# Mamba block with routed experts: expert rows scattered to a DRAM row of their own and summed at the end, in place of accumulating scatters

## The chip, the cores and the metric

The kernel runs on one core of a Trainium2 chip. The metric is the device time of one execution in microseconds (us); lower is better. All data are float32 unless a shape says otherwise.

## The reference, cut to what matters

4096 tokens (8 batches of 512) of width 128 pass a layer norm, and then two things that are added to the input: a bidirectional Mamba block, and a mixture of 16 experts of which each token takes 4.

```python
xn = _layernorm(x)
x = x + mamba(xn) + experts(xn)

def experts(x):
    logits = -sum((x - keys) ** 2) + x @ rw + rb
    topv, topi = top_k(logits, 4)
    w = softmax(topv)
    hidden = gelu(x @ w1[e] + b1[e])
    exp_out = hidden @ w2[e] + b2[e]
    return sum(w[k] * exp_out[topi[k]] for k in range(4))
```

Only the chosen experts are worked out. So each token has four expert rows of 128 numbers, made at four different places of the program, and their sum is one of the three addends of the output.

## The kernel before, in words

**Preparation (0 to about 243 us).** Tokens are normalised and routed. Each pair of token and choice gets a slot in a DRAM table `slots_d`, sorted by expert and padded to tiles of 256 rows (80 tiles). GpSimd copies the normalised rows there with 128 indirect DMAs (L817), in 16 groups; ahead of each group `tag` (L803 to L808) writes the gate weight beside the row. The row's other extra word is the token's number, written once by an iota for all tokens (L776). Unused slots carry numbers below `UNUSED`, so what they yield goes to rows that nobody reads. In the same stretch TensorE, ScalarE and VectorE prepare the Mamba inputs of all batches and SP stores them to DRAM.

Two DRAM accumulators, `acc0_d` and `acc1_d`, are filled here: the first with x (L522, L524), the second with zeros (L644 to L646, from a memset of GpSimd, L778).

**The loop.** Eight batches follow, each of 32 pairs (two states of one direction and one half of the channels). Per pair VectorE multiplies into PSUM (L1569) and scans twice (L1581), GpSimd multiplies the two states by C (L851, 128x1024), and TensorE sums the states (L1257). Between them run ten expert tiles a batch, at steps written out in `EVENTS` (`LAST` for the last batch): T (turn the rows), U0, U1 (up), D (down), and at steps 15 and 16 G and O, the output projection of the batch before. ScalarE empties the banks (`empty`); for D it scales the two halves of 128 rows by their gate weight into `yrows`, a ring of two tiles (L1026), and waits for the send of the tile two before. GpSimd then sends them (`send`, L830 to L837): two indirect DMAs with `compute_op=ADD` into accumulator `j % 2`. Ahead of that it waits until the tile before on the same accumulator has landed (`sums_landed`). For O ScalarE copies the block's output to `mixed`, and SP stores it to `mixed_d` (L689 to L692).

Everything that SP issues stands in one queue in program order: C rows (L667), weights and rows of the expert tiles, the next batch's inputs, `mixed_d`. In the last batch VectorE takes the products of pairs 22 to 31 (L1589), and SP reads `mixed_d` back for seven batches.

**The end.** SP waits for all sends of an accumulator and loads it, eight pieces of 256 KB each (L747 to L751). VectorE adds `mixed` to the first accumulator's pieces (L1628), then the second accumulator's (L1634, L1636), and for the last batch the projection from PSUM (L1639). SP stores the output, 256 KB a batch (L754).

```python
def send(b, before, j, m):
    bank_emptied(pool, s, b, "D", j, m, before)
    pool.sem_inc(s["pool_step"], 1)
    sums_landed(b, before, j)
    for a in range(SH):
        pool.indirect_dma_start(acc_d[j % W_RING], ..., compute_op=ALU.add)
```

## Time and profile before

| | |
|---|---|
| median of 3 runs | 1092.48 us (1090.7 to 1092.59) |
| the profiled execution | 1092.9 us, of which 1091.1 us are the span from the first to the last instruction |
| VectorE (DVE) busy | 1029.2 us, 94% |
| ScalarE (ACT) busy | 940.0 us, 86% |
| TensorE (PE) busy | 932.0 us, 85% |
| GpSimd (POOL) busy | 907.3 us, 83% |
| mean granted TensorE clock | 0.947 of full |

Busy shares are averages over preparation, loop and end. In the rows below, "idle before <- X" is the time an engine stood still before an instruction and what ended it; SPq is the queue of DMAs that SP issues; a row with xN stands for N instructions in a row. A row's duration of a merged group runs from the first start to the last end.

### The profile page before, as it was taken

Reading aid. Unit: us, or ns where it says so; the run is one execution under the profiler, and the core shown is the slowest. Engines: PE = TensorE matmul, PEld = TensorE weight load, DVE = VectorE, ACT = ScalarE, POOL = GpSimd, SP = SyncE. Lnnn points to the kernel's source line nnn. Section 1 sums busy time; section 2 is a strip of 40 time slices with the busy share of each in tenths; the row PEclk is TensorE's granted clock in tenths of the full one; section 3 lists DMA queues with packets and bytes.
Section 4 is the critical chain, followed back from the end, with each engine's and each line's share of the span. In section 5 each row is a group of like instructions: output and inputs, shape, how many; then the busy total and the mean of one; then the engine's idle time right before and its main releaser. Section 6 shows DMA issues by size and latency. Waiting matters only on the chain. (4 is left out here: it accounts for less than half of the span.)

```text
span 1091.1 us, 21878 instructions
## 1 busy us (share of the span) xinstructions
PE 932.0 (85%) x5866; PEld 732.8 (67%) x5866; DVE 1029.2 (94%) x1361; ACT 940.0 (86%) x1755; POOL 907.3 (83%) x567
## 2 busy tenths in 40 slices
PE   5478888857789999989999889899999999988894
PEld 2233333326678788878878777788788878877783
DVE  7889999779999999999999989999999999988896
ACT  4258989979899999989999989899899989988950
POOL 4278888766689999999999998989999999988862
PEclk9678989778999999999999999999999999999996
DMA  9956676677566877787687767776877777666658
GB/s 305 377 191 242 241 280 226 225 267 233 177 176 181 233 197 187 205 218 196 165 225 196 201 171 219 205 192 180 238 191 185 211 210 201 164 167 170 188 114 243
DMA packets 153107, 228.87 MB, mean 210 GB/s; under 512 B 36300, under 2 KB 98028, under 8 KB 147700
## 3 DMA queue, kind: packets, MB, share of 16 engines
q1 hardware_dynamic: 125844, 208.39, 60.0%
q0 software_dynamic: 27136, 19.02, 12.3%
q8 instruction: 51, 0.84, 0.3%
q14 instruction: 76, 0.62, 0.2%
HBM read 161.84 MB, written 69.64 MB: 212 GB/s over the span
## 5 line engine op out<-in xcount | busy, mean ns | idle before, releaser
L1581 DVE TENSOR_TENSOR_SCAN arena<-arena,ps 128x512 f32<-128x512 f32 x512 | 598.2, 1202 | 2.8 <-issue 1.4
L851 POOL TENSOR_TENSOR arena<-arena 128x1024 f32<-128x1024 f32 x246 | 527.0, 2472 | 44.5 <-DVE arena L1581 44.4
L1081 ACT ACTIVATE arena<-delta,a_neg 128x511 f32<-128x511 f32 x512 | 341.3, 728 | 6.3 <-DVE arena L1581 3.2
L836 POOL DMA_INDIRECT acc_d<-yrows,tags x160 | 253.1, 1582 | 46.5 <-issue 36.8
L1257 PE MATMUL ps<-ident,arena 128*128 128x128 f32 x2048 | 270.6, 276 | 3.5 <-DVE arena L1589 3.5
L1569 DVE TENSOR_TENSOR ps<-du,ps 128x512 f32<-128x512 f32 x352 | 232.8, 677 | 18.0 <-PE ps L1321 15.9
L1257 PEld LDWEIGHTS ps<-ident,arena 128*128 128x128 f32 x2048 | 233.0, 142 | 15.6 <-DVE arena L1589 4.0
L817 POOL DMA_INDIRECT slots_d<-arena,pos x128 | 148.4, 1159 | 37.1 <-issue 35.1
L1286 PE MATMUL ps<-w,arena 128*128 128x128 f32 x1248 | 174.6, 283 | 3.0 <-ACT arena L1049 3.0
L1286 PEld LDWEIGHTS ps<-w,arena 128*128 128x128 f32 x1248 | 154.4, 192 | 12.8 <-issue 3.8
L1278 PE MATMUL ps<-rowsT,w 128*128 128x256 f32 x640 | 155.8, 387 | 8.3 <-ACT arena L1031 7.6
L999 ACT ACTIVATE arena<-arena 128x256 f32<-128x256 f32 x320 | 145.4, 510 | 0.0
L1278 PEld LDWEIGHTS ps<-rowsT,w 128*128 128x128 f32 x640 | 119.2, 193 | 28.7 <-ACT arena L1031 9.2
L1020 ACT ACTIVATE arena<-ps,w 128x256 f32<-128x256 f32 x312 | 123.4, 477 | 5.4 <-PE ps L1278 5.1
L1318 PE MATMUL ps<-ident,arena 128*128 128x128 f32 x640 | 94.5, 278 | 16.5 <-DVE arena L1581 12.5
L1026 ACT ACTIVATE yrows<-ps,tags 128x128 f32<-128x128 f32 x160 | 49.9, 365 | 49.2 <-PE ps L1288 34.4
L1318 PEld LDWEIGHTS ps<-ident,arena 128*128 128x128 f32 x640 | 74.0, 143 | 21.2 <-DVE arena L1581 13.7
L1049 ACT ACTIVATE arena<-arena 128x1024 f32<-128x1024 f32 x78 | 79.1, 1054 | 0.2
L1321 PE MATMUL ps<-parts,sel 128*128 128x512 bf16 x176 | 59.3, 390 | 12.9 <-DVE arena L1581 12.9
L1271 PE MATMUL ps<-ident,rows 128*128 128x128 f32 x160 | 33.3, 290 | 37.1 <-ACT arena L1020 22.5
L1477 DVE SCALAR_TENSOR_TENSOR arena<-arena,chan 128x512 f32<-128x512 f32 x96 | 64.7, 740 | 0.0
L1271 PEld LDWEIGHTS ps<-ident,rows 128*128 128x128 f32 x160 | 18.3, 141 | 52.8 <-ACT arena L1020 23.6
(154 smaller groups left out, 911.6 us busy)
## 6 DMA issues: line engine op xcount, KB each, us to landing
arena<-c_d SPq DMA_DIRECT2D x128, 512.0 KB, 4.2
w<-w_dram SPq DMA_DIRECT2D x80, 258.0 KB, 3.1
w<-w_dram SPq DMA_DIRECT2D x80, 256.0 KB
rows<-slots_d SPq DMA_DIRECT2D x80, 130.0 KB
slots_d<-delta SPq DMA_DIRECT2D x5, 2015.0 KB, 18.9
delta_d<-arena SPq DMA_DIRECT2D x8, 1024.0 KB, 4.9
du_d<-delta SPq DMA_DIRECT2D x8, 1024.0 KB, 7.9
delta<-delta_d SPq DMA_DIRECT2D x8, 1024.0 KB, 7.0
```

Of the source, the lines that this page charges most:

```text
L817: pool.indirect_dma_start(slots_d, bass.IndirectOffsetOnAxis(ap=pos[:, t * TOPK + k:t * TOPK + k + 1], axis=0), xn[:, t, :], None).then_in ...
L836: pool.indirect_dma_start(acc_d[j % W_RING], bass.IndirectOffsetOnAxis(ap=tags[:, j, a, 0:1].bitcast(I32), axis=0), yrows[:, j % W_RING, a ...
L851: nc.gpsimd.tensor_tensor(state[:, q % H_RING], state[:, q % H_RING], c_rows[:, r % C_RING], ALU.mult).then_inc(s["prod_done"], 1)
L999: last = nc.scalar.activation(scaled_du[scaled_slot(g, j)][:, t, :], duT[:, par, t, :], ACT.Identity, scale=bT[:, par, t, n:n + 1])
L1020: last = nc.scalar.activation(hidden[hidden_slot(b, j)][:, c, :], bank[:, f * S:(f + 1) * S], ACT.Identity, bias=w1[:, j % W_RING, FF + c: ...
L1081: nc.scalar.activation(decay[:, q % DA_RING, j, lo:lo + L - 1], delta[:, par, dh, lo:lo + L - 1], ACT.Exp, scale=a_neg[:, dh, 2 * g + j:2 ...
L1257: last = nc.tensor.matmul(y_ps[:, h, t * P:(t + 1) * P], state[:, q % H_RING, j, t * P:(t + 1) * P], ident[:, :], is_transpose=True, start ...
L1278: last = nc.tensor.matmul(bank[:, f * S:(f + 1) * S], w1[:, slot, c * P:(c + 1) * P], rowsT[:, :], start=True, stop=True)
L1286: nc.tensor.matmul(bank[:, a * P:(a + 1) * P], kept[:, c, a * P:(a + 1) * P], w2[:, slot, c, :], start=c == 0, stop=False)
L1318: last = nc.tensor.transpose(bank[:, t * P:(t + 1) * P], scaled_du[scaled_slot(g, j)][:, t, h * P:(h + 1) * P], ident[:, :])
L1569: nc.vector.tensor_tensor(b_ps[:, ROW[q, j], j, :], du[:, par, q % DH, :], b_row, ALU.mult)\
L1581: nc.vector.tensor_tensor_scan(state[:, q % H_RING, j, way], decay[:, q % DA_RING, j, way], b_ps[:, ROW[q, j], j, way], 0.0, ALU.mult, ALU ...
```

## The change

The two accumulators go. A DRAM table `y_d` has one row of 512 bytes per token and choice, laid out so that 16 rows (4 tokens by 4 choices) of one partition are contiguous. The sends become plain indirect copies into it; `sums_landed` goes. The row numbers now differ by choice, so `tag` writes them anew for each of the 16 groups with a small iota. The fills of the accumulators (8 MB, with the memset and two waits) go.

Since no accumulator holds x any more, GpSimd adds it: at step 16 SP loads x of the batch before (256 KB) into the second half of `gated`, ScalarE puts the block's output in the first half, GpSimd adds the two at step 21 and SP stores the sum at step 23. `mixed` is now a view of `gated`, so `gate_batch` waits for that store. The last batch's x is loaded in the last batch itself.

At the end SP waits for the last scan and product and for both send rings, loads eight pieces of 1 MB, and VectorE adds per batch the halves (128x1024), the quarters (128x512) and the block's output.

```diff
-        acc_d = [dram(f"acc{i}_d", (UNUSED + TOK, D)) for i in range(W_RING)]
+        y_d = dram("y_d", (UNUSED + TOK * TOPK, D))
...
+        mixed, residual = (gated[:, h].rearrange("p t c -> p (t c)") for h in range(NH))
...
-            sp.dma_start(acc_d[0][0:UNUSED], x_in[0:UNUSED]).then_inc(s["acc_filled"], 16)
-            for b in range(BATCH):
-                sp.dma_start(acc_d[0][UNUSED + L * b:UNUSED + L * (b + 1)].rearrange("(p t) d -> p t d", p=P),
-                             x_in[L * b:L * (b + 1)].rearrange("(t p) d -> p t d", p=P)).then_inc(s["acc_filled"], 16)
...
                     elif what == "O":
-                        bank_emptied(sp, s, b, "O", j, m, True)
+                        bank_written(sp, s, b, "O", j, m, True)
                         sp.sem_inc(s["sp_step"], 1)
-                        sp.dma_start(one(mixed_d, b - 1), mixed[:, :]).then_inc(s["mixed_out"], 16)
+                        sp.dma_start(residual.rearrange("p (t d) -> p t d", t=TPB), x_of(b - 1)).then_inc(s["residual_in"], 16)
...
+                    if q == STORE_STEP and not (isinstance(b, int) and b == 0):
+                        wait(sp, s["residual_sum"], b)
+                        sp.sem_inc(s["sp_step"], 1)
+                        sp.dma_start(one(mixed_d, b - 1), mixed).then_inc(s["mixed_out"], 16)
...
-            sp.wait_ge(s["b_ready"], len(FILLS) * BATCH)
+            sp.wait_ge(s["scan_done"], DECAYS * BATCH)
+            product_done(sp, BATCH - 1, PAIRS - 1)
+            product_done(sp, BATCH - 1, LAST_VECTOR[0] - 1)
             for i in range(W_RING):
                 sp.wait_ge(y_out[i], 16 * SH * (NTILE // W_RING))
-                for b in range(BATCH):
-                    sp.dma_start(acc[i][:, b, :], acc_d[i][UNUSED + L * b:UNUSED + L * (b + 1)].rearrange("(p t) d -> p (t d)", p=P))\
-                        .then_inc(acc_in[i][b], 16)
+            rows_of = TPB * TOPK * P
             for b in range(BATCH):
-                sp.wait_ge(s["acc_ready"], BATCH + b)
+                sp.dma_start(outs[b], y_d[UNUSED + rows_of * b:UNUSED + rows_of * (b + 1)].rearrange("(p r) d -> p (r d)", p=P))\
+                    .then_inc(acc_in[b], 16)
...
                 nc.gpsimd.tensor_copy(xn[:, own, D + 1], gates[:, own, k]).then_inc(s["tag_ready"], 1)
+                nc.gpsimd.iota(xn[:, own, D].bitcast(I32), [[L * TOPK, part // TPB], [1, TPB]], base=UNUSED + L * TOPK * (g * part // TPB) + TPB * k,
+                               channel_multiplier=TPB * TOPK).then_inc(s["tag_ready"], 1)
...
-                sums_landed(b, before, j)
                 for a in range(SH):
-                    pool.indirect_dma_start(acc_d[j % W_RING], bass.IndirectOffsetOnAxis(ap=tags[:, j, a, 0:1].bitcast(I32), axis=0),
-                                            yrows[:, j % W_RING, a, :], None, compute_op=ALU.add).then_inc(y_out[j % W_RING], 16)
+                    pool.indirect_dma_start(y_d, bass.IndirectOffsetOnAxis(ap=tags[:, j, a, 0:1].bitcast(I32), axis=0),
+                                            yrows[:, j % W_RING, a, :], None).then_inc(y_out[j % W_RING], 16)
...
+                if q == RESIDUAL_STEP and not (isinstance(b, int) and b == 0):
...
+                    wait(pool, s["residual_in"], 16 * b)
+                    nc.gpsimd.tensor_tensor(mixed, mixed, residual, ALU.add).then_inc(s["residual_sum"], 1)
...
                 dve.wait_ge(acc_in[b], 16)
+                nc.vector.tensor_tensor(outs[b][:, 0:half], outs[b][:, 0:half], outs[b][:, half:2 * half], ALU.add).then_inc(s["tail_step"], 1)
+                dve.wait_ge(s["tail_step"], 2 * b + 1)
+                nc.vector.tensor_tensor(outs[b][:, 0:half // 2], outs[b][:, 0:half // 2], outs[b][:, half // 2:half], ALU.add)\
+                    .then_inc(s["tail_step"], 1)
+                dve.wait_ge(s["tail_step"], 2 * b + 2)
+                if b == BATCH - 1:
+                    dve.wait_ge(s["tail_x"], 1)
+                nc.vector.tensor_tensor(outs[b][:, 0:half // 2], outs[b][:, 0:half // 2], own, ALU.add).then_inc(s["acc_ready"], 1)
```

Where the instructions now stand shows at two places. The first is GpSimd's routing, where the copies of the gate weights meet the scatters to the slots (L808 and L817). Before:

```order
L791 CAST sel<-arena 128x2048
L793 TENSOR_SCALAR arena<-arena,chan 128x128 x4
L808 COPY arena<-gates 128x8 x4
L817 DMA slots_d<-arena,pos 20480x130 x16
L808 COPY arena<-gates 128x8
L817 DMA slots_d<-arena,pos 20480x130 x8
```

and in the changed kernel, from the fourth copy on:

```order
L809 COPY arena<-gates 128x8
L810 IOTA arena 128x8
L820 DMA slots_d<-arena,pos 20480x130 x16
L809 COPY arena<-gates 128x8
L810 IOTA arena 128x8
L820 DMA slots_d<-arena,pos 20480x130 x8
```

An iota stands behind each of the 16 copies: four ahead of the first scatter, twelve between scatters.

The second place is the end of VectorE's program, from its last product on. Before (all adds of 128x512):

```order
L1589 TENSOR_TENSOR arena<-arena 128x1024
L1555 TENSOR_TENSOR gated<-ps,gate 128x512 x2
L1628 TENSOR_TENSOR arena<-arena,delta 128x512 x4
L1628 TENSOR_TENSOR arena<-arena,du 128x512 x3
L1634 TENSOR_TENSOR arena<-arena 128x512 x7
L1636 TENSOR_TENSOR arena<-arena 128x512
L1639 TENSOR_TENSOR arena<-arena,ps 128x512
```

and in the changed kernel, the first of eight such triples:

```order
L1591 TENSOR_TENSOR arena<-arena 128x1024
L1557 TENSOR_TENSOR gated<-ps,gate 128x512 x2
L1636 TENSOR_TENSOR arena<-arena 128x1024
L1638 TENSOR_TENSOR arena<-arena 128x512
L1643 TENSOR_TENSOR arena<-arena,delta 128x512
```

Sixteen adds of 128x512, of which the first seven wait for pieces of the first accumulator alone, became eight of 128x1024 and seventeen of 128x512 (with the projection's, L1634); each triple waits for its batch's piece of 1 MB.

## Rows read from the trace of the kernel before

**Rows 1.** Stretches: width, busy PE, PEld, DVE, ACT, POOL, then PEclk, DMA share, GB/s.

```profile
145.00:205.00 60.00, 49.49 (x106) 19.53 (x104) 58.46 (x76) 55.32 (x61) 49.01 (x43) 0.87 0.68 242
...
345.00:945.00 600.00, 551.68 (x4046) 483.11 (x4045) 588.19 (x653) 568.85 (x1155) 562.07 (x310) 1.00 0.75 200
945.00:1045.00 100.00, 88.20 (x625) 76.52 (x623) 88.72 (x99) 91.15 (x180) 81.38 (x46) 0.98 0.66 169
```

**Rows 2.** Waits of the whole run: us in total, times, longest.

```profile
POOL arena L851 <- DVE arena L1581: 44.4, 37, 11.9
...
DVE ps L1569 <- PE ps L1321: 15.9, 25, 1.7
...
DVE gated L1555 <- PE ps L1257: 6.2, 8, 2.6
```

**Rows 3.** End of the chain that ended last: start, us, what.

```profile
1069.51 5.87 DMA acc_d<-yrows,tags
...
1078.13 5.82 DMA arena<-acc_d
...
1085.43 0.69 DVE arena L1639
```

**Rows 4.** Prices on GpSimd by line: count, then ns min/median/max, first and last start.

```profile
L836 POOL DMA_INDIRECT acc_d<-yrows,tags x160: 1548/1562/2333, 307.2 to 1069.5; - x160
...
L817 POOL DMA_INDIRECT slots_d<-arena,pos x128: 954/1017/2397, 48.8 to 238.5; - x128
...
L808 POOL COPY arena<-gates x16: 192/458/1035, 47.2 to 206.3; 128x8 f32<-128x8 f32 x16
```

**Rows 5.** GpSimd's timeline in the loop: start, us, instruction, idle before.

```profile
265.44 2.00 POOL L851 TENSOR_TENSOR arena<-arena 128x1024 f32<-128x1024 f32 x1 [2.01 <-DVE arena L1581]
```

**Rows 6.** Timelines of GpSimd and VectorE where the routing scatters begin and end.

```profile
47.16 1.43 POOL L808 COPY arena<-gates 128x8 f32<-128x8 f32 x4 [21.59 <-DMA slots_d<-delta]
48.76 1.20 POOL L817 DMA_INDIRECT slots_d<-arena,pos  x1 [0.17 <-POOL arena L808]
...
238.52 0.96 POOL L817 DMA_INDIRECT slots_d<-arena,pos  x1 [0.30 <-issue]
...
46.28 0.20 DVE L1442 CAST pos<-arena 128x32 int32<-128x32 f32 x1
```

**Rows 7.** SP's wait for the scatters, and TensorE's and VectorE's first steps of the loop.

```profile
SPq L607 <- DMA slots_d<-arena,pos: 1.6, 1, 1.6
...
246.41 0.69 PE L1271 MATMUL ps<-ident,rows 128*128 128x128 f32 x2 [5.25 <-DMA tags<-slots_d]
246.89 1.06 PE L1321 MATMUL ps<-parts,sel 128*128 128x512 bf16 x2
...
248.80 1.27 DVE L1569 TENSOR_TENSOR ps<-du,ps 128x512 f32<-128x512 f32 x2
```

**Rows 8.** Timelines of ScalarE and TensorE at the last two tiles' sends.

```profile
1058.24 0.63 ACT L1026 ACTIVATE yrows<-ps,tags 128x128 f32<-128x128 f32 x2 [4.44 <-DMA acc_d<-yrows,tags]
...
1061.61 0.23 PE L1288 MATMUL ps<-b,ones 3*128 3x128 bf16 x1
```

**Rows 9.** VectorE's timeline at the end.

```profile
1069.65 1.23 DVE L1589 TENSOR_TENSOR arena<-arena 128x1024 f32<-128x1024 f32 x1
...
1073.55 2.49 DVE L1628 TENSOR_TENSOR arena<-arena,delta 128x512 f32<-128x512 f32 x4
...
1084.63 0.69 DVE L1636 TENSOR_TENSOR arena<-arena 128x512 f32<-128x512 f32 x1
```

**Rows 10.** DMA issues: tile, queue, count, KB each, median us to landing.

```profile
delta<-delta_d SPq DMA_DIRECT2D x8, 1024.0 KB, 7.0
...
arena<-acc_d SPq DMA_DIRECT2D x16, 256.0 KB, 5.1
```

**Rows 11.** Stretches in which loads to SBUF run almost alone; columns as in Rows 1.

```profile
2.00:8.00 6.00, 0.00 (x0) 0.00 (x0) 2.75 (x20) 0.00 (x0) 4.37 (x4) 1.00 1.04 294
...
1074.00:1078.00 4.00, 3.23 (x15) 2.86 (x15) 3.97 (x7) 0.96 (x2) 0.00 (x0) 0.50 1.06 379
```

More of the change, by code:

```diff
@@ L168 @@
 MIXED_FROM = 20
+RESIDUAL_STEP = 21
+STORE_STEP = RESIDUAL_STEP + 2
 LAST_TILES = [range(GROUP + 1), range(GROUP + 1, MPB)]
@@ L236 @@
 ZERO_DMAS = len(FILL)
-ZERO_ROWS = DH * L // D
-ZERO_ACC = [(at, min(ZERO_ROWS, (UNUSED + TOK - at) // P)) for at in range(0, UNUSED + TOK, P * ZERO_ROWS)]
-ACC_DMAS = 1 + BATCH + len(ZERO_ACC)
 WTS_DMAS = 7
@@ L380, in build_kernel @@
         hidden = [hidden[:, t] for t in range(GROUP)] + late
-        acc = [t[:, 0:BATCH * TPB * D].rearrange("p (b n) -> p b n", b=BATCH)
-               for t in (arena[:, TURNED_AT:turned_end], hidden_all)]
+        YW = TOPK * TPB * D
+        outs = [arena[:, YW * b:YW * (b + 1)] for b in range(BATCH - 2)] + [hidden_all[:, YW * b:YW * (b + 1)] for b in range(2)]
+        assert (BATCH - 2) * YW <= TURNED_AT and 2 * YW <= GROUP * FC * S
         scanned = [t[:, 0, :, :].rearrange("p q l -> p (q l)").rearrange("p (b n) -> p b n", b=BATCH // 2) for t in (delta, du)]
@@ L481, in build_kernel @@
         y_out = [sem(f"y_out{i}") for i in range(W_RING)]
-        acc_in = [[sem(f"acc{i}_in{b}") for b in range(BATCH)] for i in range(W_RING)]
+        acc_in = [sem(f"acc_in{b}") for b in range(BATCH)]
         block = ctx.enter_context(nc.Block())
@@ L642, in _ @@
             store_gate(1)
-            sp.wait_ge(s["zero_acc"], 1)
-            for at, n in ZERO_ACC:
-                sp.dma_start(acc_d[1][at:at + P * n].rearrange("(p r) d -> p (r d)", p=P),
-                             du[:, 0, :, :].rearrange("p q l -> p (q l)")[:, 0:n * D]).then_inc(s["acc_filled"], 16)
             store_c(0)
@@ L728, in batch @@
                         sp.sem_inc(s["sp_step"], 1)
-                    if last and MIXED_FROM <= q < MIXED_FROM + BATCH - 1:
+                    if last and MIXED_FROM <= q < MIXED_FROM + BATCH:
                         n = q - MIXED_FROM
-                        sp.dma_start(scanned[2 * n // BATCH][:, n % (BATCH // 2), :], mixed_d[n]).then_inc(s["mixed_in"], 16)
+                        if n == BATCH - 2:
+                            sp.wait_ge(s["mixed_out"], 16 * b)
+                            sp.sem_inc(s["sp_step"], 1)
+                        dst = scanned[2 * n // BATCH][:, n % (BATCH // 2), :]
+                        if n < BATCH - 1:
+                            sp.dma_start(dst, mixed_d[n]).then_inc(s["mixed_in"], 16)
+                        else:
+                            sp.dma_start(dst.rearrange("p (t d) -> p t d", t=TPB), x_of(n)).then_inc(s["mixed_in"], 16)
             for r in range(C_RING):
@@ L775, in _ @@
             nc.gpsimd.iota(filler[:, :, D].bitcast(I32), [[1, FILL_ROWS]], base=0, channel_multiplier=FILL_ROWS).then_inc(s["zero_v"], 1)
-            nc.gpsimd.iota(xn[:, :, D].bitcast(I32), [[L, BATCH], [1, TPB]], base=UNUSED, channel_multiplier=TPB).then_inc(s["ids_ready"], 1)
-            nc.gpsimd.memset(du[:, 0, :, :], 0.0).then_inc(s["zero_acc"], 1)
             pool.wait_ge(s["b2_in"], 16)
@@ L813, in _ @@
                 k, g = n // TQ, n % TQ
-                pool.wait_ge(s["tag_ready"], n + 1)
+                pool.wait_ge(s["tag_ready"], 2 * n + 2)
                 pool.wait_ge(s["pos_ready"], min(k, 1) + 1)
@@ L820, in _ @@
                     tag(n - 1 + TQ)
-            pool.wait_ge(s["acc_filled"], 16 * ACC_DMAS)
             pool.wait_ge(s["prepared"], 1)
-            def sums_landed(b, before, j):
-                half = MPB // W_RING * (b - before)
-                wait(pool, y_out[j % W_RING], 16 * SH * (half + j // W_RING))
-                pool.sem_inc(s["pool_step"], 1)
             def send(b, before, j, m):
@@ L843, in besides @@
                             send(b, before, j, m)
+                if q == RESIDUAL_STEP and not (isinstance(b, int) and b == 0):
+                    for what, j, m, before in EVENTS[MIX_STEP]:
+                        if what == "O":
+                            bank_emptied(pool, s, b, what, j, m, before)
+                    pool.sem_inc(s["pool_step"], 1)
+                    wait(pool, s["residual_in"], 16 * b)
+                    nc.gpsimd.tensor_tensor(mixed, mixed, residual, ALU.add).then_inc(s["residual_sum"], 1)
             def batch(b):
@@ L1034, in empty @@
                     else:
-                        wait(act, s["mixed_out"], 16 * (b - 1))
-                        last = nc.scalar.copy(mixed[:, :], bank)
+                        last = nc.scalar.copy(mixed, bank)
                     last.then_inc(s[f"m{m}_free"], 1)
@@ L1552, in gate_batch @@
                 dve.wait_ge(s[f"late_in{par}"], 16 * NH * (i + 1))
+                wait(dve, s["mixed_out"], 16 * b)
                 for h in range(NH):
```

39 lines of the change are left out of this document (17 added, 22 removed).

## The prediction

> **What bounds the kernel now.** I read the stretches of the loop first, then the waits, then the chain from its end backwards, then the timelines of the last 25 us and of the first 5 us of the loop.
>
> In 600 us of loop VectorE is busy 588.19 us and GpSimd 562.07 [rows 1]. VectorE's few stops are waits for TensorE, 15.9 us before its products and 6.2 us before the gate, while GpSimd waits 44.4 us for VectorE's scans [rows 2]. So VectorE sets the pace, and GpSimd is full but follows. In the last batch VectorE stands still for 100 - 88.72 = 11.3 us [rows 1].
>
> The chain that ended last closes with a send that lands 5.87 us after its start at 1069.51 (1075.38), a load that lands at 1083.95, and VectorE's last add, which ends at 1086.12 [rows 3]. From there to the end of the span (1091.1) is 5.0 us: the store of the last batch and its landing. VectorE's last product ends at 1069.65 + 1.23 = 1070.88, 20.2 us before the end of the span [rows 9].
>
> All sums below are against the profiled execution, 1092.9 us (span 1091.1 and 1.8 outside it). It lies 0.4 us above the median of the runs. A measurement of this kernel can tell some 0.2%, 2.2 us, from no change.
>
> **Removed: the fills.** 8 MB of transfers, a memset and two waits go from the preparation. VectorE's arithmetic sets that stage (58.46 us busy of 60 [rows 1]), and none of its inputs passes through the fills, so I cost their removal at nothing. One thing can come earlier: the scatters' start. GpSimd's first gate copies waited 21.59 us, until 47.16, for the slots' zero fill, behind which the fill of x stands in SP's queue and may take some of its bandwidth; the first scatter began at 48.76, and positions were ready at 46.48 [rows 6]. Without the x fill the scatters can start at most 2.2 us earlier, at least not at all.
>
> **Added: sixteen iotas.** The nearest row is the gate copy, which has the same 128x8 shape: 0.19 at least, 0.46 in the median, 1.04 at most [rows 4]. I take 0.3, nearer to the least, because an iota reads nothing. The four ahead of the first scatter cost 0 to 1.2 us, depending on whether the zero fill ends earlier; with the possible gain above I take -1.0 for the start. The twelve between scatters cost 12 x 0.3 = 3.6 us (2.3 to 6.6, the last with 0.55). So the last scatter, which started at 238.52 [rows 6], moves by about +2.6 us.
>
> Who waits for it? SP stood 1.6 us for the scatters before it could read the first tile's rows; TensorE stood 5.25 us for these rows, and only behind their turn does it fill the B rows of pair 2, whose first is done near 247.5 (246.89 plus half of 1.06), while VectorE asks for it at 248.80 [rows 7]. That is 1.3 us of slack. So the loop starts 2.6 - 1.3 = **+1.3 us** late (0 to +6).
>
> **Changed: the sends.** The accumulating send takes GpSimd 1.56 us, never under 1.55; the scatter to the slots, also 128 rows of about 512 bytes but without an add, has a least of 0.95 and a median of 1.02 [rows 4]. I take 0.96 to 1.02 for the new one: the pairing of shape and index is the same, only the add goes. Bounds: 0.95 and 1.56. That is 20 x 0.56 = 11 us of GpSimd's time per batch. In the loop it buys little, since GpSimd waits for VectorE and not the reverse: **-0.5 us** (-2 to +1).
>
> The removed `sums_landed` wait is covered already: ScalarE waits for the same landing before it writes `yrows` [rows 8].
>
> By the Trainium skill's page "DMA: Bandwidth & Descriptors", section "SDMA does more than copy", the add of an accumulating transfer is done inside the DMA engines' data stream, so it costs no compute engine anything; by that the change gives up a free sum and buys VectorE's adds below. The rows agree for VectorE and ScalarE, and differ for GpSimd if the 0.6 us are the add's price.
>
> **Added on GpSimd: seven adds of x, 128x512.** A product of 128x1024 takes 2.00 us undisturbed [rows 5], so half is about 1.0 us plus two waits for work done five steps earlier. With 11 us won per batch, nothing. If the sends don't get cheaper, the cover is the 44.4 us of waits [rows 2], and it holds too. SP waits for this add at step 23, but it already waits there for product 21; behind it stand loads that VectorE needs many pairs later. Nothing.
>
> **The end.** The new loads wait for the last scan, the last product and both rings of sends. With sends of 1.26 us instead of 1.86 (0.30 between them), the ring of two no longer holds ScalarE back by 4.44 us [rows 8]: the last tile's bank is written at 1061.84, its copy ends near 1062.5, its two sends start by 1064.7, and even with 5.87 us [rows 3] they land by 1070.6, just before VectorE's last product at 1070.88. So the loads start there. From that point:
>
> - First piece of 1 MB landed: 256 KB landed in 5.1 us, 1 MB in 7.0 us in the busy loop [rows 10]; I take 6.0.
> - VectorE, per batch 1.23 (128x1024, the product's row) + 2 x 0.69 = 2.6 us [rows 9], with 0.11 us between dependent adds (1084.63 + 0.69 to 1085.43 in rows 3 and 9), so 2.83; eight times 22.6, and 0.7 for the projection: 23.3 us.
> - The last store, as before: 5.0 us.
>
> Sum 34.3 us, where it was 20.2: **+14.1 us**. The transfer is nearly as long: eight pieces are 8.39 MB, at 379 GB/s [rows 11] 22.1 us, plus 3.4 before the first bytes (5.1 less the 0.7 that 256 KB take is 4.4, part of it behind other pieces, so I take less) and 2.8 for the last batch's adds: 28.3 against VectorE's 29.3. Seven stores of 256 KB wait in SP's queue behind the loads and are done before the last one.
>
> Bounds of this term: first piece at 4.5 us and adds at the spacing of independent ones, 2.49 / 4 = 0.62 [rows 9], give 4.5 + 8 x 2.47 + 0.6 + 5.0 = 29.9, +9.7; loads at 294 GB/s [rows 11] give 3.4 + 28.5 + 2.8 + 5.0 = 39.7, +19.5.
>
> **Sum:** +1.3 - 0.5 + 14.1 = +14.9, so 1092.9 + 14.9 = **1107.8 us**. Its own range: from 0 - 2 + 9.7 = +7.7 (1100.6) to some 1113.
>
> **Rivals.**
>
> *A: the send keeps its price.* If the 0.6 us is the index's layout or the target's, and not the add's, the ring still ends last and the loads start at 1075.38 instead of 1070.88: 4.5 us more, 1112.3 us. For it: rows 4 show two kinds of transfer that differ in more than the add. Against: neither ever took the other's least.
>
> *B: the loads set the end.* At 294 GB/s, the rate of the first loads [rows 11], the term is +19.5, so 1113.2 us. Against: those loads had short rows; the 379 GB/s were of 2 KB runs, and the new ones are of 8 KB. The Trainium skill's page "DMA: Bandwidth & Descriptors", section "Where 436 GB/s comes from", puts the limit between HBM and SBUF at about 358 GB/s per core; row 379 is above it. By that page the pieces would take an estimated 23.4 us, and the loads, not VectorE, would set the end, by some 0.3 us.
>
> *C: the relief reaches VectorE, and the kernel is faster.* GpSimd's products come earlier, so TensorE, which takes its work in order, sums them earlier and fills VectorE's banks earlier. At most all of VectorE's 15.9 + 6.2 = 22.1 us of waits [rows 2] go: 1107.8 + 0.5 - 22.1 = 1086.2 us. It decides once more than 15.4 + 2.2 = 17.6 of the 22.1 us go. Against: GpSimd is ahead and waits for VectorE.
>
> *D: nothing measurable.* Half of C's gain and a shorter end; 1090 to 1095.
>
> **How the numbers follow.** Forecast 0.71, A 0.13, B 0.10, C 0.04, D 0.02. Predicted is the forecast's 1107.8. The range 1100 to 1117 holds the forecast, A and B, with the late loop start (+4.7 more) on top of A. Faster by over 0.2%: 0.04 (C). Within 0.2%: 0.02 (D). Slower: 0.94.
>
> **What would show it.** Sends near 1.0 us at the same lines; GpSimd's waits for scans much longer than 44.4 us; VectorE's waits about the same; the last scatter near 241 and VectorE's first stop at pair 2 near 1.3 us; after VectorE's last product some 29 us to its last add, with triples 2.8 us apart and no load waited for but the first. Wrong: sends at 1.56; triples spaced by loads; VectorE's 22.1 us of waits gone; a loop that is longer or shorter by more than 3 us.

## The result, and the profile after

The changed kernel takes **1102.75 us**, the median of 4 runs (1099.56 to 1109.54); the kernel before took 1091.88 beside it (1090.70 to 1092.59). The ratio is 1.0109, 95% interval 1.0061 to 1.0157: slower by 10.9 us, where 14.9 were forecast. Run again in another comparison the ratio was 1.0151 (1.0115 to 1.0187), there 1107.29 against 1090.39, 16.9 us. Each execution is one sample: those of the kernel before lie within 2 us of each other in the first comparison, those of the changed one within 10. With more executions the first of these doesn't hold: 17 of the kernel before in the second comparison lie between 1087.42 and 1098.27, as far apart as the changed kernel's. The execution profiled first is the fastest, 1099.56 us (span 1097.7), so its trace explains +6.7 us, and the rest has to be found in slower ones.

The prices on GpSimd in the changed kernel's first profile, by line (busy us and mean ns of one, then the idle time before): the sends are L831, the adds of x L845, the routing scatters L820, the new iota L810.

```profile
L853 POOL TENSOR_TENSOR arena<-arena 128x1024 f32<-128x1024 f32 x246 | 490.2, 2002 | 114.4 <-DVE arena L1583 101.1 <-DMA arena<-c_d 10.9
L831 POOL DMA_INDIRECT y_d<-yrows,tags x160 | 161.9, 1012 | 47.0 <-issue 36.6 <-ACT yrows L1028 9.8
L820 POOL DMA_INDIRECT slots_d<-arena,pos x128 | 149.9, 1171 | 37.9 <-issue 35.1 <-POOL arena L810 2.8
L845 POOL TENSOR_TENSOR gated<-gated 128x512 f32<-128x512 f32 x7 | 8.9, 1274 | 0.0
...
L810 POOL IOTA arena<- 128x8 int32 x16 | 2.2, 136 | 0.0
```

The sends cost 1.01 us in the mean and 0.96 in the median, against a median of 1.56 [rows 4]; an add of x 1.27. GpSimd's freed time turned into waiting for VectorE's scans, 101.1 us against 44.4 [rows 2]. The steady loop, in the columns of [rows 1]:

```profile
345.00:945.00 600.00, 551.51 (x4053) 484.70 (x4052) 589.21 (x655) 569.79 (x1157) 503.32 (x317) 1.00 0.65 202
945.00:1045.00 100.00, 88.33 (x640) 76.80 (x639) 90.19 (x100) 92.66 (x182) 70.98 (x47) 1.00 0.58 176
```

GpSimd is busy 59 us less in these 600 us, VectorE 1 us more: VectorE still sets the pace. VectorE's two waits for TensorE, 15.9 and 6.2 us before [rows 2], are still these:

```profile
DVE ps L1571 <- PE ps L1322: 14.5, 25, 2.2
...
DVE gated L1557 <- PE ps L1258: 6.2, 8, 2.5
```

VectorE's end in the first profile answers to [rows 9]:

```profile
1067.39 1.23 DVE L1591 TENSOR_TENSOR arena<-arena 128x1024 f32<-128x1024 f32 x1
...
1070.68 0.69 DVE L1557 TENSOR_TENSOR gated<-ps,gate 128x512 f32<-128x512 f32 x1 [1.47 <-PE ps L1258]
1073.60 1.22 DVE L1636 TENSOR_TENSOR arena<-arena 128x1024 f32<-128x1024 f32 x1 [2.23 <-DMA arena<-y_d]
1074.86 0.69 DVE L1638 TENSOR_TENSOR arena<-arena 128x512 f32<-128x512 f32 x1
1075.58 0.69 DVE L1643 TENSOR_TENSOR arena<-arena,delta 128x512 f32<-128x512 f32 x1
1076.19 1.22 DVE L1636 TENSOR_TENSOR arena<-arena 128x1024 f32<-128x1024 f32 x1
...
1094.30 0.69 DVE L1643 TENSOR_TENSOR arena<-arena,du 128x512 f32<-128x512 f32 x1
```

The last product ends at 1068.62, 2.26 us earlier than before; one load is waited for, the first; then a triple starts every 2.59 us (1073.60, 1076.19); the last add ends at 1094.99 and the span 2.7 us later. From the last product to the end of the span that is 29.1 us, where it was 1091.1 - 1070.88 = 20.2: **+8.9 us**. The pieces land just ahead of the adds, at the rate of the second of these stretches (columns as in [rows 11]):

```profile
1069.00:1074.00 5.00, 4.21 (x19) 3.47 (x18) 1.31 (x3) 1.17 (x2) 0.00 (x0) 0.50 0.84 315
1074.00:1090.00 16.00, 3.12 (x15) 2.83 (x14) 15.59 (x20) 0.00 (x0) 0.00 (x0) 0.61 1.01 414
```

At 414 GB/s (a few stores among the loads) 1 MB takes 2.5 us, against the triple's 2.59. The last piece lands 18.9 us after its issue at 1072.3, at 1091.2, and its triple starts at 1092.31.

To split the rest I use VectorE's second gate operation after the second batch, the one that starts near 352 us in the kernel before:

```profile
352.19 0.69 DVE L1555 TENSOR_TENSOR gated<-ps,gate 128x512 f32<-128x512 f32 x1 [0.25 <-PE ps L1257]
```

and after:

```profile
352.67 0.69 DVE L1557 TENSOR_TENSOR gated<-ps,gate 128x512 f32<-128x512 f32 x1 [0.24 <-PE ps L1258]
```

That is +0.5 up to there. From there to the last product's end it is 718.69 before and 715.95 after: -2.7. With +8.9 at the end that is the profiled execution's +6.7, to rounding.

### The profile page after: what moved, and what is told of

Read it like the earlier page. It is cut to its first block and busy times, and to the rows that moved or that the text cites. A ratio compares the mean times of both kernels' runs of the same rounds, so it can differ in the third digit from the quotient of the medians.

```text
span 1097.7 us, 21811 instructions
## 1 busy us (share of the span) xinstructions
PE 936.9 (85%) x5866; PEld 734.1 (67%) x5866; DVE 1039.8 (95%) x1370; ACT 939.5 (86%) x1755; POOL 828.2 (75%) x588
## 3 DMA queue, kind: packets, MB, share of 16 engines
q1 hardware_dynamic: 124068, 206.42, 58.1%
## 5 line engine op out<-in xcount | busy, mean ns | idle before, releaser
L853 POOL TENSOR_TENSOR arena<-arena 128x1024 f32<-128x1024 f32 x246 | 490.2, 2002 | 114.4 <-DVE arena L1583 101.1
L831 POOL DMA_INDIRECT y_d<-yrows,tags x160 | 161.9, 1012 | 47.0 <-issue 36.6
L820 POOL DMA_INDIRECT slots_d<-arena,pos x128 | 149.9, 1171 | 37.9 <-issue 35.1
L1028 ACT ACTIVATE yrows<-ps,tags 128x128 f32<-128x128 f32 x160 | 49.7, 365 | 43.6 <-PE ps L1289 38.4
L1478 DVE SCALAR_TENSOR_TENSOR arena<-arena,chan 128x512 f32<-128x512 f32 x96 | 64.7, 741 | 0.0
L1272 PEld LDWEIGHTS ps<-ident,rows 128*128 128x128 f32 x160 | 19.0, 142 | 47.5 <-ACT arena L1022 22.3
```

The costliest lines, as they stand in the source:

```text
L820: pool.indirect_dma_start(slots_d, bass.IndirectOffsetOnAxis(ap=pos[:, t * TOPK + k:t * TOPK + k + 1], axis=0), xn[:, t, :], None).then_in ...
L831: pool.indirect_dma_start(y_d, bass.IndirectOffsetOnAxis(ap=tags[:, j, a, 0:1].bitcast(I32), axis=0), yrows[:, j % W_RING, a, :], None).th ...
L853: nc.gpsimd.tensor_tensor(state[:, q % H_RING], state[:, q % H_RING], c_rows[:, r % C_RING], ALU.mult).then_inc(s["prod_done"], 1)
```

## The experiments

All are measured against the kernel before, run on the same chip. Four kinds: where the spread comes from (the first), what the sends were worth (the second), what sets the end (the third, fourth and eighth), and what disturbs the preparation (the others). "Gate" below is the second gate operation of the second batch. Each run left one profile; what is said of its stages is one execution's.

### The changed kernel once more

> The changed kernel once more, for the spread of its runs (1099.6 to 1109.5 us so far, where the kernel before stays within 2 us) and for a second profile. Theory 1, the spread comes from the end: of two profiled executions the loop's gates fall within 0.5 us of each other (second gate of the last turn near 961.6 us, last product's end near 1068.6), and the difference lies between the last product and the end of the span (29.1 us in the first profile). Theory 2, it comes from the loop: the last product's end differs by as much as the spans do. If this profile too falls at the fast end of the spread (span below 1099) it tells nothing about that.

Measured: 1107.29 us (1103.32 to 1113.52), span of the profile 1105.4, so 7.7 us longer than the first. Theory 1 fell: the end takes 29.2 us, as in the first profile. The last product ends at 1076.20, 7.6 us later, which is theory 2's sign, but its place is wrong: the gate starts at 359.38 instead of 352.67, so 6.7 of the 7.7 us are there before the loop is steady. It is the **preparation**, of which neither theory spoke. GpSimd's timeline there shows what the profile of before and the first one of the changed kernel don't have, a scatter of 6.65 us:

```profile
186.09 0.40 POOL L809 COPY arena<-gates 128x8 f32<-128x8 f32 x1
186.45 0.13 POOL L810 IOTA arena<- 128x8 int32 x1
186.75 1.69 POOL L820 DMA_INDIRECT slots_d<-arena,pos  x1 [0.16 <-POOL arena L810]
188.75 1.26 POOL L820 DMA_INDIRECT slots_d<-arena,pos  x1 [0.30 <-issue]
190.31 6.65 POOL L820 DMA_INDIRECT slots_d<-arena,pos  x1 [0.30 <-issue]
197.27 1.03 POOL L820 DMA_INDIRECT slots_d<-arena,pos  x1 [0.30 <-issue]
```

and VectorE's timeline beside it:

```profile
185.22 2.35 DVE L1519 TENSOR_TENSOR delta<-arena 128x1024 f32<-128x1024 f32 x2
187.71 1.92 DVE L1473 TENSOR_SCALAR arena<-arena,chan 128x512 f32<-128x512 f32 x4
189.54 5.38 DVE L1478 SCALAR_TENSOR_TENSOR arena<-arena,chan 128x512 f32<-128x512 f32 x8
194.84 1.29 DVE L1495 TENSOR_SCALAR du<-arena 128x1024 f32<-128x1024 f32 x2
196.04 2.74 DVE L1478 SCALAR_TENSOR_TENSOR arena<-arena,chan 128x512 f32<-128x512 f32 x4
```

The long scatter starts 0.77 us after VectorE's eight operations L1478 begin and ends at 196.96, 0.83 us after the two of L1495 that follow them end (196.13). TensorE then waits for the rows that these scatters bring, 12.22 us where it was 5.25 [rows 7], and VectorE stops behind it:

```profile
254.32 0.69 PE L1272 MATMUL ps<-ident,rows 128*128 128x128 f32 x2 [12.22 <-DMA tags<-slots_d]
```

```profile
255.47 0.69 DVE L1571 TENSOR_TENSOR ps<-du,ps 128x512 f32<-128x512 f32 x1 [5.61 <-PE ps L1322]
```

The same place in VectorE's work doesn't always do this. In the first profile a scatter starts 0.77 us into such a run of eight (125.70) and takes 1.48 us:

```profile
126.47 1.48 POOL L820 DMA_INDIRECT slots_d<-arena,pos  x1 [0.31 <-issue]
```

### The kernel before with plain sends

The sums over the experts are left out here.

```diff
-    yrows[:, j % W_RING, a, :], None, compute_op=ALU.add).then_inc(y_out[j % W_RING], 16)
+    yrows[:, j % W_RING, a, :], None).then_inc(y_out[j % W_RING], 16)
```

> The kernel before with plain sends in place of accumulating ones, so the sums over experts are left out; all else (fills, two accumulators, loads and adds at the end) stays. Theory 1, the sends carried the whole gain of the loop (0.7 us by the last turn's gate and 1.6 us in the last batch): sends of 0.96 us, last product 2.3 us earlier than 1070.88, and the loads of the second ring start about 3 us earlier as the last sends land near 1065, so 1092 - 2.3 - 2 = 1087 to 1088 us. Theory 2, the gain of the loop came from leaving out the reads of the sums or the fills or from the residual's move: sends of 0.96 us but the last product within 0.5 us of 1070.88, and only the end shortens, 1089 to 1091 us. Theory 3, the send's price is its index's or target's, not the add's: sends stay at 1.56 us, 1092 us.

Measured: 1088.33 us (1085.33 to 1090.50) against 1090.39, ratio 0.9975 (0.9957 to 0.9993). GpSimd's sends by line:

```profile
L836 POOL DMA_INDIRECT acc_d<-yrows,tags x160 | 159.9, 1000 | 50.3 <-issue 37.3 <-ACT yrows L1026 12.6
```

Theory 3 falls: the price is the add's. The last product ends at 1068.36, 2.5 us earlier than before, with fills, target and the adds of x as they were: theory 1, the sends carry the loop's gain. The end takes 15.9 us instead of 20.2. The last sends no longer hold up the loads; SP issues the first load at 1060.75 us instead of 1069.07:

```profile
1060.75 9.42 SPq L750 DMA_DIRECT2D arena<-acc_d  x16
```

Against the profile of before these two make 6.8 us, but the medians differ by 2.1: the runs of before reached down to 1087.4 in this comparison, and its profile (1092.9) is one of the slower ones. The sign and the places are shown, the size of the sum isn't.

### The changed kernel with half of each load

Two of each token's four choices are left out here.

```diff
-    sp.dma_start(outs[b], y_d[...].rearrange("(p r) d -> p (r d)", p=P))
+    sp.dma_start(outs[b][:, 0:YW // 2], y_d[...].rearrange("(p r) d -> p (r d)", p=P)[:, 0:YW // 2])
```

> The changed kernel, loading only the first half of each 1 MB piece at the end (two of the four choices of each token are left out of the result); the adds are as many and as large as before. Theory 1, VectorE's adds set the end: the triples stay at 2.59 us, only the first piece lands about 1 us earlier, so about 1101.5 us against the changed kernel's 1102.75, and its runs still spread over several us if the spread is the loop's. Theory 2, loads set the end in the slower runs: the median falls to 1098 or 1099 us and the runs keep within 2 us of each other.

Measured: 1102.54 us (1099.91 to 1106.17). VectorE's timeline at the end:

```profile
1080.21 1.23 DVE L1636 TENSOR_TENSOR arena<-arena 128x1024 f32<-128x1024 f32 x1 [1.86 <-DMA arena<-y_d]
1081.47 0.69 DVE L1638 TENSOR_TENSOR arena<-arena 128x512 f32<-128x512 f32 x1
1082.19 0.69 DVE L1643 TENSOR_TENSOR arena<-arena,delta 128x512 f32<-128x512 f32 x1
1082.80 1.22 DVE L1636 TENSOR_TENSOR arena<-arena 128x1024 f32<-128x1024 f32 x1
```

Theory 1: half the bytes, the same 2.59 us from triple to triple, a first wait of 1.86 us instead of 2.23, and 28.7 us from the last product to the end instead of 29.1. VectorE's adds set the end. The runs still lie 6 us apart, and this profile too has a scatter of 6.65 us (at 124.56) and a gate at 357.74.

### GpSimd sums three of the eight batches

```diff
+POOL_SUMS = (1, 3, 5)
...
+    for n, b in enumerate(POOL_SUMS):
+        pool.wait_ge(acc_in[b], 16)
+        nc.gpsimd.tensor_tensor(outs[b][:, 0:half], outs[b][:, 0:half], outs[b][:, half:2 * half], ALU.add)
...
     for b in range(BATCH):
...
+        if b in POOL_SUMS:
+            continue
...
```

> The changed kernel with the sums of batches 1, 3 and 5 on GpSimd (adds of 2.0, 1.28 and 1.28 us each), the other five on VectorE. Theory 1, VectorE's adds set the end and the loads stand just behind them (2.47 us per piece against 2.59): VectorE now waits for loads, the last piece lands 4.8 + 7 x 2.5 = 22.3 us after the last product, then 2.6 us of adds and 2.7 of store and 0.4: 28 us in place of 29.1, so 1 to 1.5 us faster than the changed kernel, near 1101.5 us. Theory 2, the two engines hold each other up when both add: VectorE's 128x1024 add takes well over 1.22 us, and the kernel is as slow as before or slower by up to 5 us.

Measured: 1112.62 us (1103.92 to 1115.77), 5.3 above the changed kernel of the same comparison, and 33.1 us from the last product to the end. Theory 2. VectorE's 128x1024 adds in its timeline, the first and fifth without GpSimd beside them, the third and fourth with:

```profile
1074.02 1.22 DVE L1654 TENSOR_TENSOR arena<-arena 128x1024 f32<-128x1024 f32 x1 [2.26 <-DMA arena<-y_d]
...
1083.89 2.87 DVE L1654 TENSOR_TENSOR arena<-arena 128x1024 f32<-128x1024 f32 x1 [0.41 <-DMA arena<-y_d]
...
1090.62 2.77 DVE L1654 TENSOR_TENSOR arena<-arena 128x1024 f32<-128x1024 f32 x1
...
1096.65 1.21 DVE L1654 TENSOR_TENSOR arena<-arena 128x1024 f32<-128x1024 f32 x1
```

and one of GpSimd's at the same time:

```profile
1082.90 2.78 POOL L876 TENSOR_TENSOR arena<-arena 128x1024 f32<-128x1024 f32 x1
```

When the two engines add at the same time, all operands in SBUF, both take longer: VectorE's 128x512 1.63 us instead of 0.69, GpSimd's 128x1024 2.35 to 2.79 instead of 2.00. What GpSimd takes over is lost again by that.

### The kernel before, with the iotas

```diff
     nc.gpsimd.tensor_copy(xn[:, own, D + 1], gates[:, own, k]).then_inc(s["tag_ready"], 1)
+    nc.gpsimd.iota(xn[:, own, D].bitcast(I32), [[L, part // TPB], [1, TPB]], base=UNUSED + L * (g * part // TPB),
+                   channel_multiplier=TPB).then_inc(s["tag_ready"], 1)
...
```

> The kernel before with one thing of the change: the token numbers are written anew with each of the 16 tag copies (an iota of the same shape, 0.13 us and 0.17 us until the scatter), with the values they already have. Two profiles of the changed kernel with later loop starts (by 5 and 7 us) each had one routing scatter of 6.65 us that lay beside VectorE's run of eight 128x512 operations of 5.38 us; the first profile of it and two of kernels with the old preparation had none above 2.4 us. Theory 1, the scatter's stall is a matter of its phase against VectorE's operations, which the iotas shift: runs spread over 5 us or more, the median 2 to 6 us above the kernel before. Theory 2, the fills that the change took away kept the scatters from it (or the stall has nothing to do with the change): the runs stay where the kernel before is, plus up to 1.3 us for the later last scatter.

Measured: 1096.14 us (1092.58 to 1100.86) against 1091.41, ratio 1.0043 (1.0024 to 1.0063): theory 1. Sixteen instructions of 0.13 us, which write what is there already, cost 4.7 us in the median. That the runs lie 8.3 us apart says nothing, since those of the kernel before in this comparison lie 8.2 apart. The profile has a gate at 362.04 and these rows on GpSimd:

```profile
124.59 0.13 POOL L809 IOTA arena<- 128x8 int32 x1
124.89 1.69 POOL L819 DMA_INDIRECT slots_d<-arena,pos  x1 [0.17 <-POOL arena L809]
126.88 1.26 POOL L819 DMA_INDIRECT slots_d<-arena,pos  x1 [0.30 <-issue]
128.45 6.66 POOL L819 DMA_INDIRECT slots_d<-arena,pos  x1 [0.30 <-issue]
```

Not all of this profile's 9.9 us at the gate is the scatter's. Behind it VectorE stops for 5.85 us at the second pair, but VectorE's first positions were written at 49.72 us already instead of 46.28 [rows 6], ahead of the first scatter and so of every iota between scatters (more on this under the one copy). No profile of the kernel before was taken in this comparison, so whether it shares that delay is open.

### The changed kernel with the fills put back

```diff
+    sp.dma_start(y_d[0:UNUSED], x_in[0:UNUSED]).then_inc(s["acc_filled"], 16)
+    for b in range(BATCH):
+        sp.dma_start(y_d[UNUSED + L * b:UNUSED + L * (b + 1)]...).then_inc(s["acc_filled"], 16)
...
+    for at, n in ZERO_ACC:
+        sp.dma_start(y_d[UNUSED + TOK + at:UNUSED + TOK + at + P * n]...).then_inc(s["acc_filled"], 16)
...
+    pool.wait_ge(s["acc_filled"], 16 * ACC_DMAS)
```

> The changed kernel with the 4.2 MB of fills of the two accumulators put back, as writes to the new rows, with the waits for them. Prediction's step: the fills cost nothing, so the same as the changed kernel within its spread (1102 to 1107 us). Theory 1 (phase): the first scatter starts about 1.5 us later again, so the phases differ, the stalls of 6.65 us may come or go, the spread stays several us. Theory 2, missing fills are the cause of the stalls: with them back, no scatter above 2.5 us, the runs agree within 2 us, near 1100 us.

Measured: 1108.50 us (1106.71 to 1110.56), ratio 1.0152 (1.0129 to 1.0175). The fills are 8.3 MB by the queue's bytes (214.68 against 206.42 MB), not 4.2. A scatter of 6.66 us again, so the missing fills aren't the cause: theory 2 falls. All six runs are later than the changed kernel's median of 1107.29 or within 0.6 us of it, but the changed kernel itself wasn't in this comparison. In the profile the first tag copy starts at 47.61 us, 2 us later than without the fills (45.45, 45.53), as before the change [rows 6]. That is all that can be laid on the fills.

### One copy for number and gate, no iota between scatters

```diff
-    gates = sb("gates", [P, NT, TOPK])
+    pairs = sb("pairs", [P, NT, TOPK, 2])
+    gates = pairs[:, :, :, 1]
...
-    nc.gpsimd.tensor_copy(xn[:, own, D + 1], gates[:, own, k]).then_inc(s["tag_ready"], 1)
-    nc.gpsimd.iota(xn[:, own, D].bitcast(I32), ...)
+    nc.gpsimd.tensor_copy(xn[:, own, D:D + 2].bitcast(I16), pairs[:, own, k, :].bitcast(I16)).then_inc(s["tag_ready"], 1)
...
```

The numbers are written into `pairs` by four iotas ahead of all scatters.

> The changed kernel with numbers and gates kept side by side, so that one copy writes both and no iota stands in the scatter loop. Theory 1 (phase): between tags the scatters run as in the kernel before, 1.5 us earlier; the last scatter starts near 237 us where no stall falls, and the runs move as a whole by several us against the changed kernel, down to 1099 or 1100 us if the phases are clear of stalls, and as wide a spread if they aren't. Theory 2 (the iotas cost only their time): 12 x 0.3 us less on the last scatter, of which the slack before TensorE's wait leaves up to 1 us, and the spread stays as it is.

Measured: 1103.99 us (1099.92 to 1105.81). No scatter of this profile takes more than 2.42 us, as theory 1 wants; but the first started only at 50.67, after 3.47 us of waiting for the positions from VectorE, so the last started at 240.15 and not at 237. The gate stands at 356.37 all the same, and the scatters aren't why: in the first profile the last one starts at 240.20 and the gate at 352.67. VectorE itself is late here, from its positions (46.28 in the kernel before) to its first product of the loop (243.13 there), and it makes no stop at the second pair:

```profile
49.52 0.20 DVE L1447 CAST pos<-arena 128x32 int32<-128x32 f32 x1
...
246.04 0.70 DVE L1575 TENSOR_TENSOR ps<-du,ps 128x512 f32<-128x512 f32 x1 [2.04 <-issue]
```

So the 6.65 us scatter isn't the only thing that makes a loop start late. The delay arises near 21 us: beside a GpSimd cast (L798, 1.88 us) one VectorE operation L1387 of a group of five takes 2.42 us instead of some 0.3. It is the fourth, and TensorE waits 2.55 us for it; in the kernel before the fifth is held as long, and TensorE doesn't wait. The positions are written at 47.5 to 49.7 us in all four profiles of this comparison (the iotas, the fills, the one copy, the early loads) and at 46.1 to 46.5 in the other nine. Why the four differ is open.

### Two early loads

```diff
-    outs = [arena[:, YW * b:YW * (b + 1)] for b in range(BATCH - 2)] + [hidden_all[:, YW * b:YW * (b + 1)] for b in range(2)]
+    outs = [hidden_all[:, YW * b:YW * (b + 1)] for b in range(2)] + [arena[:, YW * b:YW * (b + 1)] for b in range(BATCH - 2)]
...
-    sp.wait_ge(s["scan_done"], DECAYS * BATCH)
-    product_done(sp, BATCH - 1, PAIRS - 1)
-    product_done(sp, BATCH - 1, LAST_VECTOR[0] - 1)
...
     for b in range(BATCH):
+        if b == 2:
+            sp.wait_ge(s["scan_done"], DECAYS * BATCH)
+            product_done(sp, BATCH - 1, PAIRS - 1)
+            product_done(sp, BATCH - 1, LAST_VECTOR[0] - 1)
```

> The changed kernel with the first two pieces at the end loaded into the buffer that the expert layers leave free, as soon as the last sends have landed, and only the other six after VectorE's last product. If VectorE's adds set the end and only the first landing is exposed (a 2.2 to 2.8 us stop before the first add), that stop goes and the triples stay 2.59 us apart: 2 to 2.5 us less than the changed kernel run beside it, whose spread it keeps. If the loads set the end, up to 3.5 us less; if early loads collide with the last sends or the third piece comes late, nothing.

Measured: 1102.30 us (1099.58 to 1112.84); the changed kernel itself wasn't in this comparison, so the effect is read from the profile. VectorE's timeline at the end:

```profile
1077.10 0.69 DVE L1558 TENSOR_TENSOR gated<-ps,gate 128x512 f32<-128x512 f32 x1 [1.46 <-PE ps L1259]
1077.71 1.22 DVE L1637 TENSOR_TENSOR arena<-arena 128x1024 f32<-128x1024 f32 x1
1078.96 0.69 DVE L1639 TENSOR_TENSOR arena<-arena 128x512 f32<-128x512 f32 x1
1079.68 0.69 DVE L1644 TENSOR_TENSOR arena<-arena,delta 128x512 f32<-128x512 f32 x1
1080.29 1.22 DVE L1637 TENSOR_TENSOR arena<-arena 128x1024 f32<-128x1024 f32 x1
```

The stop before the first add is gone, and from the last product's end (1075.04) to the span's (1101.8) it is 26.8 us instead of 29.1: 2.3 less, as the first theory had it. The spread of the runs (1099.58 to 1112.84) hides it in the median, and this profile has a scatter of 6.66 us too.

### The tags at other places

```diff
     for t in range(g * part, (g + 1) * part):
+        if t == g * part + 4 and n > 0 and n - 1 + TQ < TOPK * TQ:
+            tag(n - 1 + TQ)
         pool.indirect_dma_start(slots_d, ...)
-    if n > 0 and n - 1 + TQ < TOPK * TQ:
-        tag(n - 1 + TQ)
```

This alone; then with the early loads; then with the early loads and 2 in place of 4.

> The changed kernel with each later tag (copy and iota) issued four scatters further on, in the middle of a group of eight instead of behind it. All five profiles with the stall so far show the same rows: an iota, a scatter of 1.69 us that starts 2.8 us before VectorE's run of eight begins, one of 1.26 us, and then the one of 6.65 us, 0.77 us into that run; no scatter whose predecessors were others was held so long. Theory 1 (phase): with the tags elsewhere this order of rows comes up elsewhere or not at all: the profile shows either no scatter above 2.5 us and a loop start near 352 us (second batch's first gate), or the same three rows again, and the median moves by 3 us or more either way, 1099 to 1110 us. Theory 2, the stall comes from something else than the tag's place (the count of scatters since the start, say): again one scatter of 6.65 us without an iota before it.

> The early loads of the last two buffers (the stop before the first add went, 2.3 us) together with the tags in the middle of the group. If both effects stand by themselves, this is 2.3 us below the run with the tags in the middle alone. Still slower than the kernel before by the VectorE adds at the end: not below 1096 us.

> As the run before, with the tags two scatters into the group in place of four. Theory 1 (phase): another order of rows beside VectorE's run of eight, so another rate of stalls, and a median that differs from the run before by 2 us or more, or equals it if neither meets the run of eight with an iota in front; the loop and the end are the same. 1096 to 1107 us.

Measured: 1104.04 us (1102.32 to 1106.88), 1100.87 (1097.69 to 1102.94) and 1108.15 (1105.41 to 1110.05). All three profiles have one scatter of 6.65 to 6.67 us, each behind an iota, a scatter of 1.68 or 1.69 and one of 1.25 to 1.27: theory 1 in the form "the same rows again", though the 3 us by which it wanted the median to move can't be told, since the changed kernel wasn't in this comparison. Moving the tag moved the place of the long scatter and didn't avoid it. The early loads give 3.2 us between the first two, 2.3 expected; in their profiles the end takes 26.4 us instead of 29.1. Between the last two, which differ in the tags' place alone, lie 7.3 us, the ranges apart. VectorE's stop at the second pair is 11.73 us in the last and 2.45 in the one before it; with tags after two scatters GpSimd also has to wait for the landing of the rows that it overwrites:

```profile
138.10 0.97 POOL L823 DMA_INDIRECT slots_d<-arena,pos  x1 [0.30 <-issue]
141.26 0.73 POOL L810 COPY arena<-gates 128x8 f32<-128x8 f32 x1 [2.19 <-DMA slots_d<-arena,pos]
```

The tags in the middle with early loads is the best of the changed kernels, ratio 1.0066 (1.0041 to 1.0092) to the kernel before. No run pointed to a version that beats both kernels: the one that was faster leaves the sums out.

## Why the prediction was right, and where it was not

**What bounds the kernel: right.** VectorE, in the loop and at the end; GpSimd's relief became waits for scans, and rivals C and D did not come. One reading is off, and nothing in the sum hangs on it: the stretch from 945 to 1045 us, read as the last batch, begins 17 us ahead of it (the gate operation that ends the batch before starts at 962.26), and from there to the last product VectorE stands still for some 7.6 us, not 11.3. The noise was read too small as well: the kernel before alone moved by up to 10.9 us from run to run, and the first comparison's interval is 0.5% to either side, where 0.2% was to tell a change.

**The sends: right in price, too small in the loop.** Taken 0.96 to 1.02, measured 0.96 in the median and 1.01 in the mean. Rival A falls: with the same index and target as before, the plain sends in the kernel before cost 1.00. The loop's term was -0.5 (bounds -2 to +1); the first profile has -2.7 from the gate to the last product, the second -1.9 (716.82 against 718.69), the half loads -0.8 (717.86); over the ten profiles of changed kernels it is -0.3 to -2.7, and the kernel before with the iotas, which has the old sends, stays at 718.45. The lower bound was nearly reached or passed in several; the value taken was too near zero. VectorE's waits for TensorE hardly fell, so the loop as such gave little; 1.6 of the 2.3 us by which the first profile's last product is early come in the last batch, where the sends hold back ScalarE less [rows 8]: once, for 2.94 us, where the forecast had it not at all. Over the whole run ScalarE waited 14.4 us for the landing of sends before, and now, by the waits:

```profile
ACT yrows L1028 <- DMA y_d<-yrows,tags: 5.0, 2, 2.9
```

**The adds of x: right.** 1.27 us instead of 1.0, and nobody waits for them.

**The end: the step that failed, by size.** +14.1 was taken, with +9.7 as the lower bound; +8.9 was measured against the profile of before. How far below its bound that lies isn't sure: the other profile with the old sends and the old end, the kernel before with the iotas, has an end of 18.3 us instead of 20.2, and against it the term is +10.8. Against the kernel before with plain sends (15.9) the sums at the end cost 13.2. Each of the term's three parts was too dear. The first piece, taken 6.0 us after the last product, was there at 1073.60, 5.0 us after it. The triple took 2.59 instead of 2.83: the add behind an add on the same buffer costs about 0.03 us more, not 0.11 (1074.86 + 0.69 to 1075.58), and the next batch's first add overlaps the one ahead by 0.08 like any independent pair. The last store took 2.7 us, not the 5.0 of before. There the last batches' adds, and so their stores, followed each other every 0.7 us, here every 2.59, so that the last store may find less ahead of it. The ten profiles of changed kernels all have 2.7 to 3.1, half loads included, and the three with the old end 4.2 to 5.0; that the spacing is the reason is argued, not shown, but the 5.0 had no claim to be carried over. That the loads start right at the last product (1068.69) and that VectorE, not the loads, sets the end was right: rival B falls with the half loads. The forecast's margin between them was 1.0 us in all; measured it is 2.59 against some 2.5 per piece. By the limit of about 358 GB/s per core for transfers between HBM and SBUF that the Trainium skill's page "DMA: Bandwidth & Descriptors" states in its section "Where 436 GB/s comes from", the loads would have set the end; the rows show 414, and the measurement decides.

**The start: right in sign, wrong in kind.** +1.3 us was the sum of instruction times behind the scatters. In the first profile the gate is 0.5 late, but not by that term: VectorE made no stop at the second pair, and the 0.5 stands at its first product already (243.62 against 243.13). In the later profiles the gate is 5.5 us (half loads) or 7.2 us (second profile) late, 3.9 to 11.9 over the eight with a long scatter, and what did most of it had no term: a scatter that takes 6.65 us beside VectorE's work, behind which VectorE stops for 2.5 to 11.7 us at the second pair. Ten profiles of this case have the iota between the scatters, and eight of them show it; the three without the iota don't. The kernel before with the iotas alone loses 4.7 us in the median, so it is a real cost of the change beside the end's. As a remainder, not a measurement: with +8.9 at the end and about -2 in the loop, +10.9 leaves some +4 for the start in the first comparison, and +16.9 some +10 in the second. A part of the start, up to 3.4 us in one comparison's profiles, comes from VectorE's work before 33 us, for which there was no term either.

So +14.9 came between the two measured differences, 10.9 and 16.9, by luck: errors stood against each other, the end too dear by 3.3 to 5.2, the loop by some 1.5, the start too cheap by some 3 in the first comparison's median and 9 in the second's.

## What to carry to other kernels

Price a tail by its own dependent instructions and the landing of its first piece, and ask of every row that is carried over (here the 5.0 us store) what made it that long. An instruction that is added to an engine's chain costs its time, and also moves the moment at which each later instruction of that chain meets another engine's work. Three or four runs don't show how far a kernel's runs spread; take many of both kernels, and compare two profiles stage by stage before explaining the median. A scatter-add replaced by a scatter moves the adding to the end: it pays only if what the send saves is on the path, and here 80 us off GpSimd were worth 2.

## What the runs showed of the hardware

- **A scatter issued by GpSimd can be held by VectorE.** That VectorE holds it is read from when it starts and ends; no run took VectorE's operations away. In eight of the ten profiles with an iota between the scatters, and in none of the three without, one scatter took 6.65 to 6.67 us. Each time it began 0.77 or 0.78 us into VectorE's run of eight (L1478 of the changed kernel), behind an iota, a scatter of about 1.69 and one of about 1.26, and it ended 0.83 to 0.85 us after the two VectorE operations that follow the eight. The lesser delays read alike: in the second profile the one of 2.15 us at 198.60 ends at 200.75, and VectorE's L1503 beside it (198.69, 1.22) ends at 199.91, 0.84 earlier. The Trainium skill's page "SBUF — State Buffer", section "Who interferes with whom", says that a VectorE instruction with two SBUF inputs contends with a GpSimd instruction that reads SBUF, and that a DMA stalled by VectorE was one issued from GpSimd. L1478 has two such inputs, and the trace agrees so far. The length is another matter: one scatter was held over ten VectorE operations in a row, while most scatters pass beside the same eight in 0.96 to 1.5 us, in the first profile of the changed kernel even at 0.77 us into the run (1.48 us at 126.47). What makes the difference, beyond the rows that precede it, is open.
- **Two adds at the same time slow each other:** 2.87 us instead of 1.22 for VectorE's 128x1024 and 2.78 instead of 2.00 for GpSimd's beside it.
- **An accumulating scatter of 128 rows costs GpSimd 1.56 us in the median [rows 4], a plain one 0.96** (1.00 in the mean), with the same rows, index and target, in the kernel before with plain sends.
